# A latent mixture of experts: tokens sorted by expert group through DRAM, in place of all experts for all tokens

## What is computed

```python
xn      = layernorm(x)
lat     = xn @ fc1.T                       # 256 -> 128
scores  = sigmoid(xn @ gate.T)             # 32 per token
groups  = the 2 best of 4 groups of 8      # by the sums of their best scores with bias
experts = the 8 best of the 16 experts in those groups
w       = 2.5 * scores[experts] / sum(scores[experts])
routed  = sum_e w[e] * (relu(lat @ w1[e].T) ** 2) @ w2[e].T
x      += routed @ fc2.T + shared_expert(xn)
```

## Time and profile before

| | |
|---|---|
| median of 3 runs | 2880.81 us (2879.13 to 2882.3) |
| the profiled execution | 2883.24 us, its span 2881.4 |
| busy over the span | PE 92%, DVE 59%, ACT 49%, POOL 28% |
| TensorE clock granted | 9 tenths or more in 33 of 40 slices, 6 to 7 in the last four |
| DMA | 263.18 MB, 91 GB/s in the mean |

### The profile page before, as it was taken

How to read it: one execution, slowest core, us unless ns; L and a number is a source line. 1 busy time by engine, 2 the same in 40 slices (tenths; PEclk the granted TensorE clock), 3 DMA queues, 4 the chain that set the end, 5 groups by cost and what they waited for, 6 DMA issues and landing times. The chain is left out here.

```text
span 2881.4 us, 50283 instructions
## 1 busy us (share of the span) xinstructions
PE 2641.7 (92%) x17194; PEld 2121.1 (74%) x17194; DVE 1709.2 (59%) x3298; ACT 1413.6 (49%) x2605; POOL 792.6 (28%) x803
## 2 busy tenths in 40 slices
PE   7899999979979999699999999999999999995574
PEld 6444444458768888589898998999899998983452
DVE  7688888636678888655555445555544545448421
ACT  6477777756558877633333333333333333336310
POOL 3521212200052222132222222222222222223574
PEclk9799999999989999799999999999999999996766
DMA  8964646030065444322222222222222222225476
GB/s 255 211 104 64 88 63 87 5 100 3 4 215 183 189 188 175 111 60 52 60 52 57 52 62 46 52 60 52 58 52 62 49 49 59 52 52 165 108 171 128
DMA packets 413584, 263.18 MB, mean 91 GB/s; under 512 B 257952, under 2 KB 375616, under 8 KB 404608
## 3 DMA queue, kind: packets, MB, share of 16 engines
q1 hardware_dynamic: 405104, 245.69, 33.5%
q0 software_dynamic: 8256, 14.52, 3.0%
HBM read 183.93 MB, written 80.40 MB: 92 GB/s over the span
## 5 line engine op out<-in xcount | busy, mean ns | idle before, releaser
L1888 POOL TENSOR_TENSOR lin_o2sum<-lin_o2sum,lin_o 128x512 f32<-128x512 f32 x128 | 185.5, 1450 | 932.4 <-ACT lin_o L1931 932.4
L875 DVE TENSOR_REDUCE score_pm<-score_SM 128x1 f32<-128x512 f32 (+3 forms) x608 | 364.5, 657 | 81.5 <-PE score_SM L735 48.8
L829 ACT ACTIVATE score_PR<-score_SE 128x512 f32<-128x512 f32 (+1 forms) x640 | 309.9, 558 | 107.3 <-PE score_SE L763 103.7
L2121 DVE TENSOR_TENSOR C_acc<-lin_OUT,C_acc 128x512 f32<-128x512 f32 x256 | 176.4, 692 | 244.8 <-PE lin_OUT L2022 243.3
L1908 ACT ACTIVATE lin_qT<-lin_PJ 128x512 f32<-128x512 f32 x129 | 77.0, 597 | 378.8 <-PE lin_PJ L1978 371.8
L1978 PE MATMUL lin_PJ<-C_XH,lin_WH 128*128 128x512 f32 x774 | 254.8, 410 | 8.2 <-DVE lin_WL L2101 8.2
L1978 PE MATMUL lin_PJ<-C_XL,lin_WH 128*128 128x512 f32 x774 | 241.3, 393 | 0.0
L735 PE MATMUL score_SM<-A_KR,A_QR 96*128 96x512 bf16 (+3 forms) x768 | 229.4, 339 | 12.7 <-DVEq L81 9.5
L1978 PE MATMUL lin_PJ<-C_XH,lin_WL 128*128 128x512 f32 x774 | 240.6, 392 | 0.0
L763 PE MATMUL score_SE<-A_QR,A_KR 99*128 99x512 bf16 (+3 forms) x768 | 210.7, 330 | 2.0 <-ACT score_PR L829 1.5
L1936 ACT ACTIVATE lin_goh<-lin_go 128x512 fp32r<-128x512 f32 x128 | 81.0, 633 | 251.3 <-DVE lin_go L2165 251.3
(11 more groups left out here) (354 smaller groups left out, 6503.9 us busy)
## 6 DMA issues: line engine op xcount, KB each, us to landing
experts_sq<-B_roots SPq DMA_DIRECT2D x64, 1024.0 KB, 4.7
k_turned<-lin_kblk SPq DMA_DIRECT2D x113, 256.0 KB, 2.0
lin_krow<-k_turned SPq DMA_DIRECT2D x452, 64.0 KB, 2.3
A_QR<-q_parts SPq DMA_DIRECT2D x96, 128.0 KB, 6.6
A_KR<-k_parts SPq DMA_DIRECT2D x96, 128.0 KB, 6.8
kept_GU<-L_ffn_gate_up_proj SPq DMA_DIRECT2D x48, 192.0 KB, 3.1
v_rows<-inp_vt SPq DMA_DIRECT2D x32, 256.0 KB, 4.0
A_V<-v_rows SPq DMA_DIRECT2D x16, 512.0 KB, 10.8
```

What stands on the lines that cost most here:

```text
L829: nc.scalar.activation(PR[:, st % BUFS, h, 0:width], SE[:, e % RING, 0:width], ACT.Exp, scale=SCALE)\
L875: nc.vector.tensor_reduce(pm[:, n % 2, h0:h0 + nh, t, k0 // CHUNK], SM[:, count % RING, 0:nh * nk].rearrange("p (h k) -> p h k", h=nh), AX ...
L1888: nc.gpsimd.tensor_tensor(o2sum[:, c], o2sum[:, c], o2[:], ALU.add).then_inc(pool_sum, 1)
L2121: nc.vector.tensor_tensor(dst, OUT[:, half], dst, ALU.add).then_inc(dve_acc[half], 1)
```

## The change

Only chosen groups are computed. Each token goes to two of four groups, so 8192 pairs of token and group; the pairs are sorted by group into blocks of 512. In the worst split the groups fill 19 blocks, so there are always 19 passes, each with one block and the 8 experts of its group: 152 units.

In the front (each chunk's latents and roots are now one line of 161 numbers per token: 128 latents, 32 roots, the token's number):
- SP fills the 33 blocks of B_lines in DRAM with empty lines, whose token number lies past the last token. POOL splits all expert weights, 16 pieces, and SP stores them to DRAM (B_weights), instead of the split in the experts phase.
- PE turns the latents into rows, DVE copies them into the line. DVE counts the chosen groups tile by tile, PE adds the counts up, and DVE finds each pair's place (find_places). At the end it plans the passes (plan_passes: the block and the group of each).
- POOL sends the lines to their places by indirect transfers of 128 lines each, two per tile, 64 in all (send). The last 16 wait for the last roots.
- The turning and the storing of the roots go. SP stores X to DRAM (x_rows) per chunk.

In the experts phase, per pass:
- SP reads the block's number into a register, loads the lines (B_lines), reads the group's number, loads 2 MB of weights in two halves, writes the turned roots to DRAM, waits for that, and loads them spread, in two halves of 1 MB.
- PE turns the roots of the pass after next behind down 6, ACT copies them (ROOTS_AT); PE turns the next pass's latents behind down 0, ACT copies, DVE makes the low part (LATENT_AT). Both use one PSUM bank, TR.
- The projection `out` of the pass before stands behind down 3 and down 5, and DVE's `take` copies each half at 4 and 6. POOL makes the low parts of experts 1 and 3, then adds the rows into x_rows by four indirect transfers that add, and waits for them before it makes the next targets.

At the end SP waits for all adds and loads X back in four quarters, for which lnC waits. lnC no longer stores x_rows.

The core of the diff:

```diff
-def front_phase(nc, a, AO, X, LH, LL, first_w, roots, ident, out, odd, rows):
...
+REGION = T // CHUNK
+BLOCKS = GROUPS_E * REGION + 1
+PASSES = TOP_GROUPS * REGION + GROUPS_E - 1
+LINE = LAT + EXPERTS + 1
+WU = 4
+WUNITS = 2 * EXPERTS // WU
...
+def front_phase(nc, a, AO, X, first_w, views, lines_d, weights_d, x_rows, plan, ident, out, odd, rows):
...
-            for c in range(CHUNKS):
-                sp.wait_ge(act_ro, c + 1)
-                sp.dma_start(roots[c], rootT[:, c % 2]).then_inc(stored[c % 2], 16)
...
+            sp.wait_ge(pad_ready, 1)
+            for j in range(TPC):
+                blank = pad[:, j].rearrange("p (o n) -> p o n", o=1)
+                sp.dma_start(lines_d.rearrange("(k j p) n -> j p k n", j=TPC, p=P)[j],
+                             blank.to_broadcast([P, BLOCKS, LINE])).then_inc(cleared, 16)
...
+            for u in range(WUNITS):
+                m, e = u % 2, u // 2 * WU
+                sp.wait_ge(w_low, u + 1)
+                sp.dma_start(weights_d[e:e + WU, :, 2 * m * P:2 * (m + 1) * P].rearrange("e p n -> p e n"),
+                             wparts[:, u % RING].bitcast(F32).rearrange("p e h n -> p e (h n)")).then_inc(w_out[u % RING], 16)
...
+            for g in range(CHUNKS):
+                sp.wait_ge(dve_s, (g + 1) * TPC)
+                sp.dma_start(x_rows[g * CHUNK:(g + 1) * CHUNK, :].rearrange("(t p) n -> p t n", p=P),
+                             X[:, g * TPC:(g + 1) * TPC, :]).then_inc(x_stored, 16)
...
+            def send(b):
+
+                pool.wait_ge(dve_lr, 2 * b + 2)
+                pool.wait_ge(idx_ready, b + 1)
+                pool.wait_ge(roots_ready, b + 1)
+                for t in range(BT):
+                    for k in range(TOP_GROUPS):
+                        nc.gpsimd.indirect_dma_start(
+                            out=lines_d, out_offset=bass.IndirectOffsetOnAxis(ap=idx[:, b % 2, k, t:t + 1], axis=0),
+                            in_=line[:, b % 2, t], in_offset=None).then_inc(sent[b % 2], 16)
...
+            for u in range(WUNITS):
+                weight_parts(u)
+            pool.wait_ge(cleared, 16 * (4 + TPC))
+            for b in range(NBATCH):
+                send(b)
+            for j in range(2):
+                pool.wait_ge(sent[j], 16 * TOP_GROUPS * BT * NBATCH // 2)
...
-                nc.vector.scalar_tensor_tensor(root[:], inv[:], 0.5, left[:], ALU.mult, ALU.mult)\
...
+                nc.vector.scalar_tensor_tensor(line[:, b % 2, :, LAT:LAT + E], inv[:], 0.5, left[:], ALU.mult, ALU.mult)\
...
+            add_second(last, 3)
             shares(b)
-            add_second(last, 3)
+            find_places(b)
+            plan_passes()
             refined_roots(b)
...
-    COPY_AT, OUT_AFTER, ADD_AT = 2, (4, 7), (7, 10)
...
+    N8 = PER_GROUP
+    N = PASSES * N8
+    AHEAD, BUFS, HALVES = 4, 4, 2
+    HALF = N8 // HALVES
+    ON_POOL = (1, 3)
+    ON_DVE = [e for e in range(N8) if e not in ON_POOL]
+    ROOTS_AT, LATENT_AT, COPY_AT, OUT_AT, TAKE_AT = 6, 0, 2, (3, 5), (4, 6)
...
+            def lines_of(c):
+                need(sp, pe_lt, c - 1)
+                need(sp, to_set, c - 1)
+                at = sp.value_load(plan[0:1, 0, c:c + 1], min_val=0, max_val=BLOCKS - 1)
+                sp.dma_start(got[:, c % 2], lines_d[bass.ds(at * CHUNK, CHUNK), :].rearrange("(j p) n -> p j n", p=P))\
+                    .then_inc(lines_in[c % 2], 16)
+
+            def weights_of(c):
+                group = sp.value_load(plan[0:1, 1, c:c + 1], min_val=0, max_val=GROUPS_E - 1)
+                for v in range(HALVES):
+                    need(sp, pe_y, (c - 2) * N8 + (v + 1) * HALF)
+                    sp.dma_start(W[:, c % 2, v * HALF:(v + 1) * HALF].bitcast(F32).rearrange("p e k n -> p e (k n)"),
+                                 weights_d[bass.ds(group * N8 + v * HALF, HALF)].rearrange("e p n -> p e n"))\
+                        .then_inc(w_in[c % 2][v], 16)
+
+            def roots_of(c):
+                group = sp.value_load(plan[0:1, 1, c:c + 1], min_val=0, max_val=GROUPS_E - 1)
+                need(sp, act_rt, c + 1)
+                for v in range(HALVES):
+                    need(sp, sq_in[c % 2][v], 16 * (c // 2))
+                sp.dma_start(roots_d[c % 2], rT[:]).then_inc(r_out, 16)
+                sp.wait_ge(r_out, 16 * (c + 1))
+                for v in range(HALVES):
+                    need(sp, dve_z, (c - 2) * N8 + (v + 1) * HALF)
+                    src = roots_d[c % 2, bass.ds(group * N8 + v * HALF, HALF), :].rearrange("(o e) n -> o (e n)", o=1)
+                    sp.dma_start(sq[:, c % 2, v * HALF:(v + 1) * HALF].rearrange("p e n -> p (e n)"),
+                                 src.to_broadcast([P, HALF * CHUNK])).then_inc(sq_in[c % 2][v], 16)
...
+            for c in range(PASSES):
+                if c + 2 < PASSES:
+                    lines_of(c + 2)
+                if c + 1 < PASSES:
+                    weights_of(c + 1)
+                    roots_of(c + 1)
+            sp.wait_ge(added, 16 * TPC * PASSES)
+            part = TILES // len(x_back)
+            for j, back in enumerate(x_back):
+                sp.dma_start(X[:, j * part:(j + 1) * part, :],
+                             x_rows[j * part * P:(j + 1) * part * P, :].rearrange("(t p) n -> p t n", p=P)).then_inc(back, 16)
...
+            def take(c, half):
+
+                need(dve, added, 16 * TPC * c)
+                dve.wait_ge(pe_o, 2 * c + half + 1)
+                nc.vector.tensor_copy(yr[:, 2 * half:2 * half + 2, :], OP[:]).then_inc(dve_o, 1)
...
+            for c in range(PASSES):
+                for e in range(N8):
+                    weigh(c, e)
+                    if e and e - 1 in ON_DVE:
+                        low(c, e - 1)
+                    elif e == 0 and c and N8 - 1 in ON_DVE:
+                        low(c - 1, N8 - 1)
+                    if e == LATENT_AT + 1 and c + 1 < PASSES:
+                        latent_low(c + 1)
+                    if c and e in TAKE_AT:
+                        take(c - 1, TAKE_AT.index(e))
...
+                for t in (2 * half, 2 * half + 1):
+                    nc.gpsimd.indirect_dma_start(out=x_rows,
+                                                 out_offset=bass.IndirectOffsetOnAxis(ap=to[:, c % 2, t:t + 1], axis=0),
+                                                 in_=yr[:, t], in_offset=None, compute_op=ALU.add).then_inc(added, 16)
...
+            for c in range(PASSES):
+                for e in ON_POOL:
+                    low(c, e)
+                if c:
+                    add(c - 1, 0)
+                    add(c - 1, 1)
+                if c + 1 < PASSES:
+                    targets(c + 1)
...
+            for c in range(PASSES):
+                for e in range(N8):
+                    square(c, e)
+                    if e == LATENT_AT and c + 1 < PASSES:
+                        latent_high(c + 1)
+                    if e == COPY_AT and c:
+                        copy_y(c - 1)
+                    if e == ROOTS_AT and c + 2 < PASSES:
+                        roots_copy(c + 2)
...
+            for n in range(N):
+                c, e = divmod(n, N8)
+                if n + AHEAD < N:
+                    up(*divmod(n + AHEAD, N8))
+                down(c, e)
+                if e == LATENT_AT and c + 1 < PASSES:
+                    turn_latent(c + 1, c + 2)
+                if c and e in OUT_AT:
+                    out(c - 1, OUT_AT.index(e))
+                if e == ROOTS_AT and c + 2 < PASSES:
+                    turn_roots(c + 2)
...
-                  (x_rows.rearrange("(t p) n -> p t n", p=P), X[:]),
```

More of the change, by code:

```diff
@@ L1556, in _, with latent_low @@
-            with dve.Fori(0, CHUNKS) as g:
-                for e in range(E):
-                    weigh(g, e)
-                    if e and not on_pool(e - 1):
-                        low(g, e - 1)
-                    if e in ADD_AT:
-                        half = ADD_AT.index(e)
-                        add(2 * g + half, (g + CHUNKS - 1) % CHUNKS, half)
+            def latent_low(c):
+                dve.wait_ge(act_lh, c + 1)
+                nc.vector.tensor_tensor(LL[:, c % 2], TR[:], LH[:, c % 2].bitcast(F32), ALU.subtract).then_inc(dve_ll, 1)
@@ L1627, in _ @@
+            targets(0)
+            for c in range(PASSES):
[6 more added lines that the diff above has]
+                    targets(c + 1)
+            for half in range(2):
+                add(PASSES - 1, half)
+            pool.wait_ge(added, 16 * TPC * PASSES)
         @block.scalar
         def _(act):
-            give_credit(act, act_h, act_hh, act_y)
@@ L1660, in _ @@
+            copy_y(PASSES - 1)
         @block.tensor
         def _(pe):
[L1662 to L1673 removed]
@@ L1690, in out, with turn_roots, turn_latent @@
-            def out(n, half):
+            def turn_roots(c):
+                pe.wait_ge(lines_in[c % 2], landed(c))
+                need(pe, dve_ll, c)
+                for j in range(TPC):
```

(23 more changed lines are left out.)

523 lines of the change are left out of this document (270 added, 253 removed).

## The result

The change made the kernel slower: 3009.04 us (median of 4, 3006.73 to 3011.45) against 2881.56, a ratio of 1.0443 with a 95% interval of 1.0424 to 1.0461. The prediction was 2974, range 2905 to 3040: right in sign and inside the range, 35 us short.

What follows compares the result with a forecast made beforehand. PE bounds the kernel before; the changed passes were to be bound by a chain of waits, 22.0 us each. 2883.2 + 59.5 (experts) + 34 (front) = 2976.7 profiled, the median 2.4 below: 2974, range 2905 to 3040.

Steps and rivals of the forecast that it cites:

- The pass: Experts stage: a chain of waits between engines plus two surcharges makes each pass 22.0 us, against PE's own 13.6.
- The chain of turns and takes: Experts pass: steps right behind the PE work they need, 19.3 us, plus 1.1 for hand-overs, 20.4 a pass.
- The two surcharges: Added to each pass's 20.4 us: 1.4 for a lower clock and 0.2 for slower lows on DVE.
- The clock: Experts passes: granted clock 0.80 with PE busy two thirds, +1.4 us a pass (nothing at 1.00, +3.7 at 0.60).
- The lows on DVE: Experts passes: DVE's lows slow down while POOL reads SBUF, 726 ns against 0.69 us, so 0.2 for six.
- rival C: Experts: SP's chain binds, weights awaiting the last down with old ones; 3.7 us late, pass 24.1, 3012; chance 0.14.
- The front, step that failed: Front: weight splitting and 10.9 MB of fill on nearly idle POOL and DMA engines cost nothing, within +34 us.
- The prediction's own sign of being wrong: Front: the prediction is wrong if POOL's sends hold the front up in its body; no size given.
- Rival B: Front: the scatters cost what the adds cost, +32 us, 3006; chance 0.11.
- Ramp and tail: Experts stage's ends: ramp 14.7 us to the start, tail 15, and 5.4 for X's first quarter to come back.
- Rival A: Experts: waits don't bind, engines catch up between turns, a pass runs at PE's 13.6 us, 2823 in all; chance 0.11.
- Its low end: Whole time: front at +18 (−16), clock at 1.00 (−29), one turn of four covered (−22): 2907, so 2905.

Runs made afterwards that it cites:

- e4: The change with scatter targets made at the pass's start from four buffers, and slack for the turnings of roots and latents; 2924.8 us.
- e1: The change with POOL sending the first batch's 16 scatters after 6 of 16 weight splits instead of after all; 2982.7 us.
- e12: e9 with the takes one expert later, the adds' rows in two buffers and only expert 3's low on POOL; 2855.3 us.
- e5: e4 with outs behind down 3 and 6, later takes, adds' rows in two buffers, POOL's lows at experts 0 and 4; 2918.8 us.
- e11: e12's kernel with split weights in pieces of 8 KB a partition instead of 2 KB; 2884.2 us.
- e9: The change with the edits of e1 and e4, and the turned roots' write ahead of the weights on SP; 2887.3 us.

## Why the prediction was right, and where it was not

- **The pass.** 22.0 forecast, 21.99 measured, but that they meet is luck. The chain of turns and takes stands: 20.4 forecast, 20.2 to 20.3 in the two kernels without SP's delay, and e4 takes 2.6 out of it by two turns' slack, as its expectation had it. The two surcharges were wrong. The clock: 0.94 with PE busy 275.59 of 368, where I took 0.80 from the earlier trace rows. The lows on DVE: their mean was

```profile
L1715 DVE TENSOR_TENSOR experts_hl<-experts_h,experts_hh 128x512 fp32r<-128x512 f32 x114 | 78.3, 687 | 26.4 <-ACT experts_hh L1799 23.7
```

  against 726 before; in the pass shown POOL's low (1011.76 to 1013.04) ran beside two weighs and the next low of DVE began at 1013.19. In the whole stage one of the 114 lows ran beside a low of POOL, for 0.06 us, so the rule of the Trainium skill that I weighed ("SBUF — State Buffer", Who interferes with whom) had hardly an occasion here. (Where the two did meet in the kernel before, three lows that overlapped by 0.7 to 0.9 us took 1.26 to 1.45 in place of 0.69.) In place of the surcharges, 1.6 together, stood SP's 1.7 a pass, which I had as rival C, there 3.7 above the chain of 20.4.
- **Rival C** was there, at another place: I had SP waiting for the down that frees the weights. It waited for the adds' landing ahead of the lines and for the write behind the weights, and the row that I cited for a queued transfer was of the right kind: the 128 KB that landed after 15.6 behind the store of 4 MB landed after 6.1 in the changed kernel, which has no such store there.
- **The front, step that failed:** "The weight splitting and the 10.9 MB of fill lie on POOL and the DMA engines, nearly idle there ... nothing." They were idle, but the work was ahead of the sends on the same two queues. I priced the work and not what is queued behind it. The prediction's own sign of being wrong, that "POOL's sends hold the front up in its body", came true here. The sum had the last root 11 us later (7 + 4), it came 37.3 later; e1 takes 21.8 of that back (17.6 in the mean of all traces), and what makes the rest was not tried. From the last root to the experts it is 30.9 against 29.8, again by errors that cancel: 2.0 until the third batch's sends are through, 19.9 for the last sixteen (24.8 in the sum), 9.1 for landing and barrier (5).
- **Rival B** fell. A send of 128 rows took 0.96, as a gather of 96 took 0.93; with the issue 1.27, not 1.55, and an add 1.56 where 96 rows took 1.44. In these pairs the price hangs on the instruction far more than on its rows.
- **Ramp and tail:** 16.7 (14.7 forecast) to DVE's first weigh, the spread roots being asked for 7.5 us after the write's issue; from the last copy of the sum to lnC 20.9 (15 + 5.4).
- **Rival A** lost, but its pass exists: e12 runs 14.4 a pass in its trace, near PE's own 13.6 to 14. Fewer units do pay, 0.7% here, once the waits for other engines, SP's queue and the adds are mostly out of the way.
- **The range.** Its low end takes 29 us away for the clock at 1.00; the clock's surcharge is 18 x 1.4 = 25, the other 4 are the lows'. The range does not hang on it.

## What to carry to other kernels

Before calling added work hidden because its engine is idle, list what stands behind it on that engine's queue and who waits for that; the same holds for a small write queued behind large loads. Give steps that hand one pass's data round several engines slack, as the loop that they join has it; shortening one of two chains of nearly equal length gains little until the other goes too (13 us alone, 49 behind the other edit here), so test them in pairs. After each wait that is removed, read the trace again, for the next one may be of the same size, as e5 and e11 showed. And before calling a sum right because its total was met, check its terms one by one.

## What the runs showed of the hardware

- An indirect transfer kept POOL hardly longer with a third more rows: 0.96 for 128 rows sent, 0.93 for 96 gathered; 1.56 and 1.44 where it adds. The rows of these pairs are not of the same kind, so this bounds the price per row and does not measure it.
- A 64 KB write landed in 2.1 us where it was asked for ahead of the weights (e9) and in 7.3 behind their 2 MB (the change). POOL's adds beside those loads landed after 6.9 in the median, where the earlier trace rows has 3.5 for a gather late in the kernel. The Trainium skill ("DMA: Bandwidth & Descriptors", Issuing engines are not separate DMA queues) says that transfers of SP and POOL run on the same 16 engines and interleave; these numbers fit that, without proving it.
- Four fills of 2656.5 KB each, in lines of 644 bytes, kept SP's queue issuing for 44.91 us.
- The granted clock was 0.94 in the passes of the change, with PE busy 75% of the time and waiting in many short gaps; in its front, after 22.8 us without a matmul, it was 0.50 from 753 to 755, the lower level.
